# Mamba layer laid out as 8 channels x 16 states on the partitions, its inputs copied there through DRAM; state sums and softmax denominators moved to TensorE; the layer's first phase scheduled by itself

## What is computed

```python
# layer 0, per image b: x (4096, 128)
xh, z = split(x @ W_in)                      # 256 inner channels d each
xh = silu(causal_conv_k2(xh))
dt_low, B, C = split(xh @ W_x)               # 8, 16, 16
dt = softplus(dt_low @ W_dt + b_dt)          # (4096, 256)
h = exp(dt_t[d] * A[d, n]) * h + dt_t[d] * B_t[n] * xh_t[d]   # 256 x 16 states, over t
y_t[d] = sum_n h[d, n] * C_t[n] + xh_t[d] * D[d]
x = silu(group_norm((y * silu(z)) @ W_out)) + x
# layer 1, attention: scores through tanh, strictly causal, softmax without maximum
t = tanh(f[:, None, :] + g[None, :, :] + b1)       # 4096 x 4096 x 16
e = exp(t @ w2 + b2) * tril(-1);  t = x + (e / (e.sum(-1) + 1e-10)) @ layernorm(x)
# layer 1, experts: softmax over the sequence, top 8 positions per expert, two matmuls, scattered back
```

## Time and profile before

| | |
|---|---|
| runs | 14669.48, 14661.69 us, median 14665.58 us |
| the profiled execution | 14662.6 us, its span 14660.9 us |
| busy: PE, DVE, ACT, POOL | 9050.9 (62%), 9564.8 (65%), 10019.6 (68%), 4164.0 us (28%) |
| mean granted TensorE clock | 0.780 of full speed |
| DMA | 226.64 MB, mean 15 GB/s |

### The profile page before, as it was taken

How to read it: one execution, slowest core, us unless ns; L and a number is a source line. 1 busy time by engine, 2 the same in 40 slices (tenths; PEclk the granted TensorE clock), 3 DMA queues, 4 the chain that set the end, 5 groups by cost and what they waited for, 6 DMA issues and landing times. The chain is left out here.

```text
span 14660.9 us, 117816 instructions
## 1 busy us (share of the span) xinstructions
PE 9050.9 (62%) x46698; PEld 2975.0 (20%) x46698; DVE 9564.8 (65%) x10322; ACT 10019.6 (68%) x6491; POOL 4164.0 (28%) x1466
## 2 busy tenths in 40 slices
PE   2235655756566665766657566666656666577775
PEld 0001112211222112221222112221122212122323
DVE  8977777477755777477683777657774776832143
ACT  1116776777767776876768687677767677689990
POOL 2323332133422333133331333213331233311110
PEclk5557777877778777877779777787778878799996
DMA  0000000000000000000000000000000000000005
GB/s 7 3 16 3 5 3 23 13 3 3 3 24 11 3 3 5 23 11 5 5 17 17 5 3 3 24 11 3 3 3 24 11 3 6 13 17 28 25 14 211
DMA packets 102727, 226.64 MB, mean 15 GB/s; under 512 B 12889, under 2 KB 13281, under 8 KB 99617
## 3 DMA queue, kind: packets, MB, share of 16 engines
q1 hardware_dynamic: 102176, 219.11, 4.4%
HBM read 143.58 MB, written 75.50 MB: 15 GB/s over the span
## 5 line engine op out<-in xcount | busy, mean ns | idle before, releaser
L1229 ACT ACTIVATE arena<-arena 128x2048 f32<-128x2048 f32 (+15 forms) x4096 | 7006.2, 1783 | 506.7 <-PE banks L614 450.4
L614 PE MATMUL banks<-arena,w2b 128*32 128x512 f32 (+5 forms) x36864 | 5550.1, 695 | 1778.2 <-ACT arena L1237 625.3
L1302 POOL TENSOR_TENSOR arena<-arena 128x2048 f32<-128x2048 f32 x512 | 2335.2, 4561 | 4103.4 <-DVE arena L900 4103.4
L889 DVE TENSOR_TENSOR_SCAN arena<-arena 128x1024 f32<-128x1024 f32 x1024 | 3386.2, 3346 | 39.6 <-issue 2.2
L614 PEld LDWEIGHTS banks<-arena,w2b 128*32 128x32 f32 x36864 | 1558.4, 130 | 5288.0 <-issue 2444.7
L557 PE MATMUL banks<-arena,sel 96*128 96x512 bf16 x2048 | 840.8, 465 | 2677.7 <-DVE arena L900 2425.0
L1198 ACT ACTIVATE arena<-arena,An 128x1024 f32<-128x1024 f32 x1024 | 1116.5, 1138 | 1179.3 <-DVE arena L889 1132.2
L1330 POOL TENSOR_TENSOR arena<-arena 128x2048 f32<-128x2048 f32 (+15 forms) x368 | 1310.2, 3560 | 1197.1 <-ACT arena L1247 1176.5
L1042 DVE TENSOR_TENSOR arena<-arena,banks 128x512 f32<-128x512 f32 (+1 forms) x512 | 334.6, 653 | 1890.8 <-PE banks L635 1672.2
L1237 ACT ACTIVATE arena<-arena 128x1024 f32<-128x1024 f32 (+7 forms) x512 | 1066.7, 2116 | 681.7 <-DVE arena L1027 680.2
L876 DVE TENSOR_TENSOR arena<-arena,banks 128x1024 f32<-128x1024 f32 x1024 | 1201.4, 1215 | 106.1 <-PE banks L557 105.8
(11 more groups left out here) (166 smaller groups left out, 5563.7 us busy)
## 6 DMA issues: line engine op xcount, KB each, us to landing
arena<-in_x_dram SPq DMA_DIRECT2D x136, 256.0 KB, 2.7
t_scratch<-arena SPq DMA_DIRECT2D x128, 256.0 KB, 2.1
arena<-in_L_ffn_weight_dram SPq DMA_DIRECT2D x32, 1024.0 KB, 14.3
arena<-t_scratch SPq DMA_DIRECT2D x64, 256.0 KB, 3.4
xt_scratch<-arena SPq DMA_DIRECT2D x64, 256.0 KB, 2.0
arena<-xt_scratch SPq DMA_DIRECT2D x64, 256.0 KB, 3.1
arena<-t_scratch SPq DMA_DIRECT2D x8, 2048.0 KB, 11.1
out_dram<-arena SPq DMA_DIRECT2D x8, 2048.0 KB, 16.6
```

The costliest lines, as they stand in the source:

```text
L614: mm = e.matmul(TR[32 * q:32 * q + 32, c - sh, l - 512 * c:512], w2b[:, m, :], tile[:, l - org:512 * c + 512 - org], start=(m == 0), stop= ...
L889: e.tensor_tensor_scan(Un[:, h, :], En[:, h, :], Un[:, h, :], ST[:, h, n:n + 1] if c else 0.0, ALU.mult, ALU.add).then_inc(scan_ve.h, scan ...
L1229: e.activation(TH[plan.slot[key][q]][:, lo:SUP], Fq[:, I * SUP + lo:I * SUP + SUP], ACT.Tanh, bias=gcol(b, jb, 4 * q + m)).then_inc(tanh.h ...
L1302: e.tensor_tensor(Y, Y, U[n % 2], ALU.add).then_inc(y_po.h, y_po.tick(tuple(k)))
```

## The change

**Layout of the scan.** A scan instruction now covers 8 channels x 16 states on the 128 partitions and 1024 positions. The 256 channels are 32 groups, and with 4 chunks there are 128 waves w per image, one 128x1024 scan each; before there were 64 pairs (chunk, n) of two such scans. B and C are the same for all channels, so they lie in SBUF for a chunk (`BR`, `CR`), and dt and dt*x have to be repeated 16 times: they are written to DRAM, and each wave loads both, 512 KB each, into rings of NDT = 4 and NDX = 6 tiles, with each source row read for 16 partitions. The sum over n is now a sum over partitions: a matmul of float32 with a 0/1 matrix `sel`, 32 output rows each, which adds up four waves a row block in bank 5. GpSimd's adds onto Y go, and so does the three-part bf16 broadcast.

```diff
-                yield 2.5, ("n1", b, c, n)
-                yield 4.7, ("n2", b, c, n)
-                yield 2.5, ("n3", b, c, n)
+        for w in range(n + 4):                       # n = 128 waves
+            if w + 1 < n:
+                todo += [(0.1, ("q", b, w + 1)), (1.2, ("u", b, w + 1))]
+            if w < n:
+                todo.append((2.4, ("h", b, w)))
+            if 1 <= w <= n:
+                todo.append((1.2, ("c", b, w - 1)))
...
+            if w < n and w < n - NG32:
+                todo.append((0.1, ("k", b, w)))
+            if w % 2 == 1 and w >= 3 and w - 3 < n:
+                todo.append((0.1, ("y", b, (w - 3) // 2)))
+            if w % 2 == 1 and w >= 1:
+                todo += [(0.1, ("r", b, x)) for x in (w + 3, w + 4) if 4 <= x < n]
...
+                elif op == "u":                      # VectorE
+                    e.tensor_tensor(DXR[w % NDX], DXR[w % NDX], BR[c % 2], ALU.mult)
+                elif op == "h":
+                    e.tensor_tensor_scan(DXR[w % NDX], DTR[w % NDT], DXR[w % NDX], ST[:, g:g + 1] if c else 0.0,
+                                         ALU.mult, ALU.add)
+                elif op == "c":
+                    e.tensor_tensor(DXR[w % NDX], DXR[w % NDX], CR, ALU.mult)
...
+                elif op == "q":                      # ScalarE
+                    e.activation(DTR[w % NDT], DTR[w % NDT], ACT.Exp, scale=An[:, g:g + 1])
...
+                elif op == "y":                      # TensorE, after the c of both waves
+                    for half in range(2):
+                        for w in (2 * p, 2 * p + 1):
+                            lo = 32 * (gg // 4 + 2 * half)
+                            mm = e.matmul(TR[lo:lo + 32, i, :], sel[:, gg % 4, :], DXR[w % NDX][:, chunk(half)],
+                                          start=(gg % 4 == 0), stop=(gg % 4 == 3))
...
+                elif op == "r":                      # SyncE
+                    if w >= NDT:
+                        q_.wait_ge(scan_ve, (b, w - NDT))
+                    e.dma_start(DTR[w % NDT], dtd[b % 2][part].unsqueeze(1).to_broadcast([8, NS, T]))
...                                                  # waits for the y of wave w - 6
+                    e.dma_start(DXR[w % NDX], dxd[b % 2][part].unsqueeze(1).to_broadcast([8, NS, T]))
...
-                elif op == "n3":                     # GpSimd
-                    e.tensor_tensor(Y, Y, U[n % 2], ALU.add)
```

```diff
+            if b + 1 < NB:
+                X = (self.conv(1) if b == 0 else []) + self.scan(b + 1) + self.norm(b + 1)
...
+            if b + 2 < NB:
+                X = self.conv(b + 2)
...
+            act = 4 * w * 0.000833 + (0.8 if w > 1024 else 0.25)
+            own = 0.65 if w > 1024 else 4 * (0.21 + 0.00052 * w) + 0.4
+            weight.append(max(0.92 * act - own, 0.15 * act))
```

**Denominators.** `esum` and its GpSimd adds go. A step `dn` after the `av` steps of each pair of key blocks multiplies the exp rows with a 128x32 matrix of ones (up to 8 matmuls, four row blocks of bank 4), and one VectorE instruction adds bank 4 onto `DEN`:

```diff
-                        e.tensor_tensor(esum[:, cs:SUP], esum[:, cs:SUP], EX[jb % 2][:, cs:SUP],
-                                        ALU.add)
+                            mm = e.matmul(TR[row(c):row(c) + 32, i, l - 512 * c:512], ones[:, :],
+                                          EX[m][:, l:512 * c + 512], start=(m == 0), stop=last)
```

1087 lines of the change are left out of this document (595 added, 492 removed).

## The result

| | before | after |
|---|---|---|
| median of the runs | 14665.58 us | 15853.59 us (15831.26 to 15875.92) |
| ratio | | 1.081 (95% interval 1.074 to 1.088) |
| busy DVE, ACT, PE, POOL in the profiled execution | 9565, 10020, 9051, 4164 us | 8214, 9982, 10063, 444 us |
| mean granted TensorE clock | 0.780 | 0.812 |

The account below looks back on a forecast made before the run. Seven Mamba stages of about 1400 us were taken as bound by neither DVE nor ACT all the time. 960 + 1115 + 6 x 1025 + 6 x 375 + 313 + 860 + 293 + 360, plus 2, gave 12300 us; range 11850 to 13500.

Parts of the forecast that it names:

- start: Opening part, where Mamba of image 0 runs alone: 960 us (930 to 1100), against 1108 before.
- stage 1, image 0: Image 0's stage 1, with Mamba's scans and also conv(1): 1115 us (1035 to 1290), against 1391 before.
- stage 1, images 1 to 6, each: Stage carrying attention and Mamba's scans: bound by ACT, 1025 us (995 to 1200), against 1407 before.
- stage 0, images 0 to 5, each: Stage that gets the convolution of image b + 2: 375 us (345 to 430, the latter by today's busy ratio).
- images 6 and 7, tail: Image 6's stage 0 at 313, image 7's stages at 860 and 293, the tail at 360 us.
- the price of the wave loads: Scan loop: a wave's 1 MiB of loads takes 2.5 to 5.5 us, hidden within attention; start taken at 5.1 a wave.
- the rule that says so: Rival for wave loads: outermost size 8 means half the engines serve them, 6.2 us a wave, 12500 us in all; chance 0.15.
- Slower than before: Rival for wave loads: still dearer, 1024 P + 6000 exceeds 14661 us from P = 8.5; chance 0.04.
- P: Price in us of one wave's loads of dt and dt*x.
- the rival before it: Rival: wave loads become the bound throughout, a stage 1 128 P plus about 230 us; 13450 at P = 7.2; chance 0.08.
- A wave's loads are hidden if P is below the wave's period: Scan loop within attention: a wave is due every 6.6 us, so loads of 2.5 to 5.5 us cost nothing there.
- dn: Denominators' step in stage 1: adds 16 x 0.65 = 10 us to DVE.

Follow-up runs that it names:

- the kernel without loads: Changed kernel without the wave loads behind an image's first four dt and six dx loads, waits for scan and state sum in their place; 13481.41 us.
- the three edits: Changed kernel with states outermost (16 engines), side steps ahead of S, and dn no longer right in front of ex; 12833.55 us, ratio to before 0.875.

## Why the prediction was wrong

The terms of the sum, each against the changed kernel, us (forecast, measured, and what the kernel without loads has):

| term | forecast | after | without loads |
|---|---|---|---|
| start | 960 | 1208 | 1002 |
| stage 1, image 0 | 1115 | 1600 | 1265 |
| stage 1, images 1 to 6, each | 1025 | 1350 | 1039 |
| stage 0, images 0 to 5, each | 375 | 514 | 515 |
| images 6 and 7, tail | 1826 | 1883 | 1889 |

The miss is 3573 us: 248 + 485 + 6 x 325 + 6 x 139 + 57.

- **The step that failed first is the price of the wave loads**, "between 2.5 and 5.5 us ... within attention a wave is due every 6.6 us and the loads are hidden". The bounds came from rates of transfers on 16 engines. The form used runs on 8, and at 129 GB/s when issued back to back, which is 8.1 us a MiB; in the kernel a wave takes 6.6 us in the start, and a wave's 32 packets an engine at 242 ns come to 7.7 us in stage 1. The loads were not hidden in any stage that has them; they make up 2370 us of the miss. I had the rule that says so, gave it 0.15 and a price of 6.2 us, by halving 340 GB/s. What came is the rival *Slower than before*, to which I gave 0.04. That halving was the second error in the same step: a packet on these 8 engines also takes 200 ns in the start, 242 in stage 1 and 259 alone, not the 159 of an undisturbed engine. With P = 8.1 the working of the last rival, 1024 P + 6000, gives 14300. Stages 0, left at 375 there, add 830, and the rest lies in the stages 1: image 0's 1600 and the others' 1350 where 128 P + 230 gives 1270. Late issue comes there on top of the rate. (For P = 7.2 the same working gives 13370, not the 13450 that stands in the rival before it; and all lower bounds add up to 11833, not 11850.)
- **"A wave's loads are hidden if P is below the wave's period"** is also wrong as a step. It takes a load as issued when the tile is free in DVE's order. SyncE issued the load of dt*x behind a wait for y on TensorE, which stood behind S and so behind four tanhs. I had costed what the DMA takes and not what stands ahead of its issue. Moving y and the other side steps ahead of S returned 1680 us with the eight engines kept, 172 of them in each stage 1 of images 1 to 6, 320 in image 0's and some 350 in the stages 0, which have no such loads.
- **Stage 0**: "plus 20 for a chain of short steps spread over 64 tanh steps". The chain cost 159, not 20. Of that, 58 us were steps standing behind S; 81 above the forecast remain, were not brought down by spreading, and stay open. The ratio bound of 430 was exceeded too. Image 0's stage 1, which carries the same steps, is 150 us over its 1115 even without loads (1265), and 1157 with 16 engines and the steps ahead of S.
- **dn** was costed as 10 us of VectorE. What it cost was its place in the queue, in front of ex: 28 us in image 7's stage 1, of the 45 by which that stage missed its 860.
- **Right**: the scan at 2.29 us (2.33) and GpSimd's adds as the cause; ACT 930 and DVE 800 in stage 1 (934 and 777); DVE 225 and ACT 318 in stage 0 (225 and 311); and the stage "bound by ACT at 1025", which the kernel with 16 engines and the side steps ahead of S has at 1029. TensorE, taken as no more than 861 us in a stage 1, is busy for 887 in the changed kernel and for 751 with the three edits. A wave was forecast at 4.9 us and takes 4.58 where nothing waits. The start is 42 us dearer than forecast even without loads, although its waves are not: its first scan begins at 257 us there, where the constants, conv(0), logarithms, copies and first loads were put at 204.

So the change removed what it was to remove. Of the 16% that were forecast it would bring 13% with another numbering of the partitions and another place for TensorE's side steps.

## What to carry to other kernels

Before a broadcast load goes into a plan, price its own form: how many engines its outermost size allows, and where on the partitions each of them writes. An estimate from other transfers' rates was off here by a factor of 2.6 (340 against 129 GB/s): 2 from the number of engines, the rest from slower packets. And for a load through a ring ask not only how long it takes but what stands ahead of its issue: each queue that frees the tile, with everything in front of it there. When one engine fills nine tenths of a stage on paper, short dependent steps deserve their place in the order more than their duration does.

## What the runs showed of the hardware

- With the compute engines idle, a 4096-byte packet from DRAM into SBUF took 159 ns in the undisturbed forms and a median of 600 ns where 16 engines loaded 16 partitions (form M).
- Eight engines gave 197 GB/s (8 x 8 into 64 partitions) or 129 (8 x 16 into 128) from 8 source rows; why the second is slower stays open.
- Going from 8 to 16 engines raised the rate of back-to-back loads from 129 to 232 GB/s and the packet from 259 to 282 ns; in the kernel it was worth 1530 us.
- GpSimd's tensor adds beside VectorE's scans cost the kernel before 1100 us, more than the 890 us by which the scans themselves got shorter.
- A scan of 128x1024 took 2.31 us with no GpSimd add beside it and 4.48 us with one; where only adds of exp rows were left, the scans beside them were longer by 2.10 us for 2.27 us of the add inside them.
